# Three row blocks in place of three interleaved rows in the attention stage's placed operands

## The reference

```
x = x + tanh(g_xattn[0]) * mlstm(layernorm(x), ctx, ctx)          # stage A
x = x + tanh(g_ffn[0])   * lora_ffn(layernorm(x))                 # stage B
x = x + tanh(g_xattn[1]) * attention(layernorm(x), ctx)           # stage C
x = x + tanh(g_ffn[1])   * mixture_of_experts(layernorm(x))       # stage D

# attention, 16 heads of 16 features, all 256 context tokens:
scores = einsum('bhsd,bhtd->bhst', q * 16**-0.5, k)
y = einsum('bhst,bhtd->bhsd', softmax(scores), v) @ Wc
```

## Time and profile before

| | us |
|---|---|
| median of three runs | 1496.33 |
| the profiled execution, its own time | 1498.18 |
| its span (first to last instruction) | 1496.6 |
| stage C inside the span | about 480 to 890 |
| PE busy in the span | 1239.7 (83%) |
| DVE / ACT busy | 843.4 / 674.0 |

### The profile page before, as it was taken

One profiled execution on the slowest core, in us unless ns is written; L12 is line 12 of the kernel. 1 busy time (PEld: TensorE's weight loads), 2 busy tenths in 40 slices (PEclk: granted clock), 3 DMA queues, 4 the chain that ended last, 5 costly groups with the idle time before them and its releaser, 6 DMA issues. The chain is left out here.

```text
span 1496.6 us, 28865 instructions
## 1 busy us (share of the span) xinstructions
PE 1239.7 (83%) x9374; PEld 1017.2 (68%) x9375; DVE 843.4 (56%) x2009; ACT 674.0 (45%) x1430; POOL 398.0 (27%) x529
## 2 busy tenths in 40 slices
PE   1959894699996578989899857779489999998798
PEld 0336662498996456666666536779478888887798
DVE  2337785845453557677777636556644444443566
ACT  0347782246452146655655633334633333332444
POOL 1126674213121101011101011667011111110763
PEclk9969897699999679999999977899789999999899
DMA  4245452000001524323432215676012112221664
GB/s 142 86 147 176 173 202 65 0 0 0 0 0 45 99 61 92 98 71 86 101 78 69 45 46 185 236 251 231 28 50 66 63 63 64 69 63 53 229 212 148
DMA packets 91066, 145.61 MB, mean 97 GB/s; under 512 B 12532, under 2 KB 69160, under 8 KB 88668
## 3 DMA queue, kind: packets, MB, share of 16 engines
q1 hardware_dynamic: 80428, 116.81, 25.8%
q0 software_dynamic: 9984, 27.28, 5.8%
q10 hardware_dynamic: 560, 0.30, 0.1%
HBM read 86.71 MB, written 31.85 MB: 79 GB/s over the span
## 5 line engine op out<-in xcount | busy, mean ns | idle before, releaser
L1127 DVE TENSOR_REDUCE c_mx<-c_s 128x2 f32<-128x512 f32 x256 | 164.3, 684 | 83.6 <-PE c_s L1256 83.5
L1050 ACT ACTIVATE c_probs<-c_t 128x512 f32<-128x512 f32 x256 | 139.0, 595 | 12.2 <-PE c_t L1278 8.9
L1935 POOL DMA_DIRECT2D de_z<-d_z_rows x71 | 38.2, 538 | 278.7 <-issue 278.7
L659 ACT ACTIVATE b_g_full<-b_hid,b_b 128x512 f32<-128x512 f32 x64 | 44.2, 691 | 102.9 <-PE b_hid L34 88.0
L1972 DVE TENSOR_TENSOR de_zt_lo<-de_zt_ps,de_zt_hi 128x256 fp32r<-128x256 f32 x71 | 30.2, 425 | 102.8 <-ACT de_zt_hi L1949 102.8
L1954 ACT ACTIVATE de_g<-de_h_ps 128x512 f32<-128x512 f32 x71 | 42.5, 598 | 94.8 <-PE de_h_ps L2016 94.8
L1959 ACT ACTIVATE de_gt_hi<-de_gt_ps 128x512 fp32r<-128x512 f32 x71 | 42.4, 598 | 94.2 <-PE de_gt_ps L2022 94.2
L1256 PE MATMUL c_s<-c_kt,c_qt 48*128 48x256 f32 x512 | 67.1, 342 | 19.7 <-DVE c_mx L1127 19.0
L32 PE MATMUL de_h_ps<-de_w_hi,de_zt_hi 128*128 x142 | 63.1, 444 | 23.4 <-DVE de_zt_lo L1972 16.9
L32 PE MATMUL de_y_ps<-de_w_hi,de_gt_hi 128*128 x284 | 80.2, 282 | 1.4 <-DVE de_gt_lo L1977 1.4
L34 PE MATMUL de_y_ps<-de_w_hi,de_gt_lo 128*128 x284 | 80.2, 282 | 0.0
(11 more groups left out here) (337 smaller groups left out, 4111.7 us busy)
## 6 DMA issues: line engine op xcount, KB each, us to landing
a_mb<-a_maxima SPq DMA_DIRECT2D x16, 1024.0 KB, 4.7
de_z<-d_z_rows POOLq DMA_DIRECT2D x71, 128.0 KB, 2.3
d_y_rows<-de_ys SPq DMA_DIRECT2D x71, 128.0 KB, 1.8
c_kt<-c_k_hi SPq DMA_DIRECT2D x64, 128.0 KB, 3.1
c_qt<-c_q_hi SPq DMA_DIRECT2D x64, 128.0 KB, 3.3
dr_zt_in<-d_zt_kept SPq DMA_DIRECT2D x16, 512.0 KB
d_w_lo<-in_w SPq DMA_DIRECT2D x16, 512.0 KB
dc_zt<-d_zt_kept SPq DMA_DIRECT2D x16, 512.0 KB, 4.8
```

The source lines that it names most:

```text
L659: act.activation(g_full[:, m % GR, :], hid[m % HR][:], ACT.Gelu, bias=b1[:, m:m + 1]).then_inc(gelu_full, 1)
L1050: act.activation(probs[h % PR][:], t_ps[k][:], ACT.Exp).then_inc(exp_done, 1)
L1127: dve.tensor_reduce(mx[n % 2][:, :, k, p:p + 1], s_ps[h % SB][:], AX.X, ALU.max).then_inc(max_done, 1)
```

## The change

The same DMAs are issued in the same order, from the same source, with the same size and semaphores. Their destination rows differ: part r of a half goes to 16 adjacent rows, 16 r to 16 r + 15, in place of every third row. `K3` is 48, `DH` is 16 and `PARTS` is 3. The order of the 48 rows is again the same in both operands, so the matmuls sum the same products in another order. No instruction is added, removed or moved on any engine.

```diff
                 for r in range(PARTS):
                     for k in range(2):
                         if parts[r] == part:
-                            row = HALF * k + r
-                            sync.dma_start(dst[n % R][row:row + K3 - r:PARTS, :, :].bitcast(F32),
+                            row = HALF * k + DH * r
+                            sync.dma_start(dst[n % R][row:row + DH, :, :].bitcast(F32),
                                            split[part][:, k, :].bitcast(F32)).then_inc(placed[n % R], 16)
```

## The result

| | kernel before | changed kernel |
|---|---|---|
| median in one comparison (4 runs each) | 1494.68 us | 1536.91 us |
| lowest to highest | 1492.52 to 1498.18 | 1529.17 to 1541.07 |
| the profiled execution (its span) | 1498.18 (1496.6) | 1538.21 (1536.7) |
| mean granted clock of PE | 0.916 | 0.898 |

The change makes the kernel slower: 1.0266 times the time, 95% interval 1.0226 to 1.0305, over all 21 runs of the changed kernel on record (1525.58 to 1547.38 us, median 1534.37). The prediction was 1496.5 us with a range of 1490 to 1510; what happened is nearest to its rival 1, named there with 1540 us.

What follows compares the result with a forecast made beforehand. PE was taken as nearest to the bound in stage C, with its waits deciding. The profiled 1498.18 us + 0 (landing) + 0 (clock), that execution standing 1.85 us above the runs' median of 1496.33, gave 1496.5 us, range 1490 to 1510.

Steps and rivals of the forecast that it cites:

- rival 1: Stage C, last q landing: halves don't overlap, each of 12 DMAs takes 1.37 us; +34 to +83 us, 1540 named; chance 0.19.
- the pace holds and only the last DMA's own tail grows, by 1.37 - 0.75 = 0.6 us: Stage C placing burst: last landing 0.6 us later, under the 1.3 us of room, so cost 14 elements x 0.
- the halves at rows 0 and 64 running side by side: Placing DMAs alternate halves; two at once were to move 2 x 96 = 192 GB/s, as much as the present 175 to 199.
- eight adjacent rows at 48 GB/s: Stage A's `a_gates<-ag_g_rows` read, 6 GB/s for a row, used as upper bound: 1.37 us for one DMA instead of 0.75.
- the lower end: Last q landing: 0.6 us later was taken, near the lower end, because today's stream keeps pace with rows shared at random.
- a whole element ahead of the scores: Stage C: k's DMAs were said to be placed that early, behind the same landing of q, so nothing hangs on them.
- the whole placing moves 87 GB/s on average, under even 96: Argument against rival 1: average placing rate in stage C is below the 96 GB/s bound for 16 adjacent rows.
- a tail of 0.3 us: Port estimate for one placing DMA: 1.2 us against 0.9, so 0.3 us later, under the 1.3 us of room; cost 0.
- the room of 1.3 us: Stage C, PE's wait for `c_yt_lo` after the scores: a later q landing eats this first, up to 1.3 us per element free.
- The clock: PE's falls to 1.2 GHz every second element, 0.66 us each: six or seven more or fewer, +4.6 to -4.6 us, taken as 0.
- rival 2: Stage C, PE's idle stretch is cut in two and clock falls go: 4.6 us less, 1492 us; chance 0.08.
- rival 3: Placing DMAs unchanged, landing at 3.1 to 3.7 us as before, 1496.3 us; chance 0.68 together with the forecast.

Runs made afterwards that it cites:

- p1: Kernel before plus twelve sets of six 128 KB DMAs ahead of stage A, row spacing varied: 1590.2 us; 16 adjacent rows 107 GB/s, halves in turn 125.
- p2: Kernel before plus six DMA sets ahead of stage A, rows three apart or adjacent: 183 GB/s in the kernel before's pattern, 117 in the changed kernel's.
- e2: Kernel before with only k's rows put in adjacent blocks, q's left three apart (output differs): 1498.24 us, ratio 1.0021 to the kernel before.
- e3: Kernel before with only q's rows put in adjacent blocks, k's left three apart (output differs): 1498.77 us, ratio 1.0030 to the kernel before.
- the fillers: Useless matmuls per element where PE stands: 24 in the changed kernel, 1521.40 us, ratio 1.0158; ten in the kernel before, 1492.71 us, ratio 0.9964.
- a2: The changed kernel run again, unaltered, in one comparison with the filled kernels: 1535.25 us, ratio 1.0244 to the kernel before.

## Why the prediction was wrong

*The step that failed:* "the pace holds and only the last DMA's own tail grows, by 1.37 - 0.75 = 0.6 us". It rested on the halves at rows 0 and 64 running side by side. They hardly do: p1 and p2 give 104 to 107 GB/s in one half and 117 to 125 in turn. So every one of the 12 DMAs is slower, not the last one. The changed kernel's own window over the later half of the burst that starts at 680.86 shows the pace:

```profile
689.00:695.00 6.00, 3.83 (x42) 2.44 (x41) 4.74 (x12) 3.77 (x8) 2.43 (x4) 1.00 1.15 125
```

At 125 GB/s a DMA takes 131.1/125 = 1.05 us, and k's six (6.3 us) aren't written when q's first is issued, 5.36 us after k's. (SP issues the next element's context load at 690.05; p2's rate for this pattern alone, 117 GB/s or 1.12 us, doesn't contain it.) The burst is written 12 x 1.05 = 12.6 us after its start, where it was 4.76 + 6 x 0.75 = 9.3 us: 3.3 us more, against 3.4 measured at the landing. The prediction worked this case out as its rival 1, at 1.37 us for a DMA and 3.7 to 7.2 us at the landing. Mechanism and signs were those it named, landings over 5 us, `c_yt_lo` gone, elements of 24 us and more; its price for one DMA, 1.37 us, was too high by some 20 to 30% (1.05 to 1.12). That its 1540 us lies so near the time is in part luck: its DMA was too dear and it held nothing for the clock. With the measured 3.4 us at the landing its own sum gives 1496.3 + 14 x (3.4 - 1.3), or 1526 us.

*What misled:* the row, eight adjacent rows at 48 GB/s, was read rightly as 6 GB/s for a row (p1: 107/16 = 6.7). But it was then left aside for the lower end. The sentence that k is placed "a whole element ahead of the scores" was wrong: k at 668.65, q at 673.41 and the scores at 680.80 belong to one element, so a slower k pushes q's landing, and in e2 k alone made it 1.6 us later. The argument "the whole placing moves 87 GB/s on average, under even 96" was of no use: a burst of 12 with a reader waiting at its end is not an average. The Trainium skill's sentence was used for one DMA by itself, a tail of 0.3 us. Further on, that page of the Trainium skill (SBUF — State Buffer, section "Can I just issue two DMAs to hit both halves?") has two concurrent DMAs at partitions 0 and 64 at only 6% over one; the prediction didn't weigh it. The runs agree in kind, with 14 to 17% for adjacent rows, and not in size for rows three apart, 44%.

*The step that held:* the room of 1.3 us behind the wait. e2 and e3 land 1.6 and 1.8 us later and cost 0.2 to 0.3%.

*The clock:* taken as 0 with 4.6 us on either side, a second term mis-sized. It was larger. With PE still for 3.3 us the clock falls to the lower level in every element (0.91 in both windows, against 0.92 and 1.00 in turn), and the fillers take back 13.9 us of it after and 3.5 before: a term of 10.4 us. The prediction priced a fall at 0.66 us from two neighbouring elements and let only its number vary, not its length.

*The sum as the runs have it:* 14 elements x (3.4 - 1.3) = 29 us for the landing past the room, which the filled kernels show without the clock as 1521.40 - 1492.71 = 28.7 us, and 10.4 us for the clock: 39 us, against 39.0 (a2), 39.7 (all 21 runs) and 42.2 us (the four runs of the table). The match is closer than its parts: in the twelve elements the filled kernels differ by 1.8 us each and not by 2.1, so the room was nearer 1.6 us than 1.3, and 14 x 1.8 is 25 us. In their profiled executions stage D's first indirect DMA stands at 956.99 against 931.00, 26.0 us apart.

*What held besides:* DVE, ACT and POOL do the same work in the same time; nothing is lost at the stage's start (551.74 against 552.85); rival 2, the clock turning faster, had the wrong sign, and rival 3, nothing at the DMAs, is refuted by the landings.

*Open:* how a DMA holds the engines is inferred from the rates, and no row shows it. Each set of p1 and p2 ran once, six DMAs long. Why 32 adjacent rows stay at 152 GB/s was not tried.

## What to carry to other kernels

For a transfer into SBUF count, DMA by DMA, how many of its rows fall into one group of four neighbours and the four rows 32 further on, and spread them two or four apart; a neighbour DMA to other rows makes up for little where rows are adjacent (14 to 17% here). When a burst lands just ahead of its reader, price the pace of the whole burst, take off the wait that stands behind, and expect parts of a change that are free alone to cost in full together. PE's idle stretch of 3.3 us cost its length and a slower clock after it, and matmuls of no use in it gave the clock's part back.

## What the runs showed of the hardware

- Three rows apart is not free either: 126 to 131 GB/s in one half, against 203 to 210 two, four or eight apart. Only the turns of the halves bring it to 181 to 183.
- 32 adjacent rows, with 4 KB each, reach 152 GB/s where 16 rows two apart with 8 KB each reach 204, although the fullest group gets the same 16 KB.
- A second issuing queue to the other half gives 121 GB/s, no more than one queue in turn (125, 119).
- Ten matmuls of no use per element made the kernel before 0.36% faster [0.18%, 0.54%]; the mean clock from 555 to 820 us is 1.00, where it was 0.97.
- At a clock of 1.00 the scores' matmuls take 279 ns in the median whether their 48 rows are interleaved or in blocks.
